# Second feed-forward layer of a four-layer model: first halves in four PSUM banks, second halves first, both products ahead of both clips

## What is computed

```python
def swiglu(x):
    g, l = jnp.minimum(x[..., ::2], 7.0), jnp.clip(x[..., 1::2], -7.0, 7.0)
    return g * jax.nn.sigmoid(1.702 * g) * (l + 1.0)
def body(acc, p):
    ew1, eb1, ew3, eb3, ew2, eb2, ce = p
    h = swiglu((xt @ ew1 + eb1) * (xt @ ew3 + eb3))
    return (acc + ce[:, None] * (h @ ew2 + eb2), None)
```

## Time and profile before

| | |
|---|---|
| median of the runs | 2266.28 us |
| the profiled execution, its span | 2269.38 us, 2267.8 us |
| busy over the span: TensorE, VectorE, ScalarE, GpSimd | 79%, 74%, 47%, 37% |
| first pass of the shared expert, last addition of the stage | 955.6 us, 1284.7 us |
| VectorE busy in that stretch | 301.1 us |
| TensorE busy in it | 288.8 us |
| granted TensorE clock: span, routed experts | 0.89, 1.00 |

### The profile page before, as it was taken

How to read it: one execution, slowest core, us unless ns; L and a number is a source line. 1 busy time by engine, 2 the same in 40 slices (tenths; PEclk the granted TensorE clock), 3 DMA queues, 4 the chain that set the end, 5 groups by cost and what they waited for, 6 DMA issues and landing times. The chain is left out here.

```text
span 2267.8 us, 46290 instructions
## 1 busy us (share of the span) xinstructions
PE 1800.0 (79%) x16408; PEld 1306.8 (58%) x16408; DVE 1674.2 (74%) x3948; ACT 1071.9 (47%) x2023; POOL 838.7 (37%) x632
## 2 busy tenths in 40 slices
PE   6999965888888975499999567878887659997756
PEld 3777742555555643377777434555554448886544
DVE  5999996776666757789999846988999672224674
ACT  4888843455545422144444324555565323332532
POOL 3000017755555401134443343455444219911111
PEclk8999987999999997699999867988898769998877
DMA  3111102000000000100000174444444250000000
GB/s 117 54 53 45 59 14 77 18 18 18 18 18 17 18 1 5 25 12 13 24 23 12 20 240 130 145 150 145 156 150 142 65 213 20 19 0 7 1 1 21
DMA packets 130613, 129.41 MB, mean 57 GB/s; under 512 B 76565, under 2 KB 107131, under 8 KB 129682
## 3 DMA queue, kind: packets, MB, share of 16 engines
q1 hardware_dynamic: 129522, 126.78, 18.8%
q10 hardware_dynamic: 928, 0.47, 0.1%
HBM read 78.59 MB, written 40.81 MB: 53 GB/s over the span
## 5 line engine op out<-in xcount | busy, mean ns | idle before, releaser
L2825 ACT ACTIVATE l2a_pr<-l2a_ps_s,l2a_nm 128x512 f32<-128x512 f32 x256 | 174.1, 686 | 140.9 <-DVE l2a_nm L2748 138.3
L529 ACT ACTIVATE l0a_pr<-l0a_sm,l0a_nm 128x512 f32<-128x512 f32 x256 | 185.0, 723 | 47.7 <-DVE l0a_nm L398 46.4
L398 DVE CUSTOM_DVE_ANT_0 l0a_sm<-l0a_ps_s,l0a_tb 128x512 f32<-128x512 f32 x256 | 174.9, 684 | 25.1 <-PE l0a_ps_s L613 18.5
L1703 POOL TENSOR_TENSOR l1f_h<-l1f_lm,l1f_sg 128x512 f32<-128x512 f32 x72 | 92.5, 1284 | 184.8 <-DVE l1f_lm L1767 184.8
L2748 DVE TENSOR_REDUCE l2a_nm<-l2a_ps_s 128x2 f32<-128x1024 f32 x128 | 156.7, 1224 | 4.4
L2755 DVE STREAM_TRANSPOSE l2a_tt<-l2a_pr 128x1024 f32<-128x1024 f32 x128 | 158.0, 1234 | 0.9 <-ACT l2a_pr L2825 0.8
L621 PE MATMUL l0a_ps_p<-top_c_ident,l0a_pr 128*128 128x128 f32 x1024 | 155.7, 274 | 0.0
L621 PEld LDWEIGHTS l0a_ps_p<-top_c_ident,l0a_pr 128*128 128x128 f32 x1024 | 129.0, 141 | 22.0 <-issue 0.9
L1829 ACT ACTIVATE l1f_csb<-l1f_ps_c,l1f_b3e 128x512 f32<-128x512 f32 x128 | 88.1, 689 | 107.5 <-PE l1f_ps_c L1615 107.3
L2082 ACT ACTIVATE l2f_h<-l2f_ps_h 128x512 f32<-128x512 f32 x128 | 76.5, 599 | 131.6 <-PE l2f_ps_h L1615 125.4
L2049 DVE SCALAR_TENSOR_TENSOR l2f_acc<-l2f_ps_y,l2f_comb,l2f_acc 128x128 f32<-128x128 f32 x112 | 31.5, 345 | 134.6 <-PE l2f_ps_y L2123 134.6
(11 more groups left out here) (535 smaller groups left out, 5098.8 us busy)
## 6 DMA issues: line engine op xcount, KB each, us to landing
l_qband<-l2a_staged SPq DMA_DIRECT2D x16, 768.0 KB, 16.2
l2a_qb<-l_qband SPq DMA_DIRECT2D x16, 768.0 KB
l2a_sb<-l_pband SPq DMA_DIRECT2D x32, 384.0 KB
l0a_tb<-l_bias SPq DMA_DIRECT2D x16, 448.0 KB
l2a_ks<-l_k SPq DMA_DIRECT2D x16, 384.0 KB
l_pband<-l2a_pr SPq DMA_DIRECT2D x32, 192.0 KB, 8.1
l_pband<-l2a_pr SPq DMA_DIRECT2D x32, 144.0 KB, 2.4
l2f_upw<-in_L_ffn_up_weights SPq DMA_DIRECT2D x9, 512.0 KB, 11.2
```

Source lines behind the costliest of these rows:

```text
L398: v.tensor_tensor_reduce(sm[j % 4][:, :], ps_s[j % 2][:, :], tb[slot][:, off:off + N][:, ::-1], -1.0, 3e38, ALU.add, ALU.min, nm[:, j % 4: ...
L529: a.activation(pr[j % 4][:, :], sm[j % 4][:, :], ACT.Exp, bias=nm[:, j % 4:j % 4 + 1], scale=-1.0).then_inc(m["p_ready"], 1)
L2825: a.activation(pr[slot][:, 2 * (g % 2) + u, :], ps_s[g % 2][:, u, :], ACT.Exp, bias=nm[:, g % 2, u:u + 1], accum_out=rs[:, n % 2, 2 * (g % ...
```

## The change

TensorE makes `c` first, then `a`; each has its own semaphore. `ps_a` gets four banks (one for each quarter), `ps_c` keeps two, `csb` gets four tiles. The two banks come from `ps_t` and `ps_g`, which now lie in the banks of `ps_y`. `c` of quarter m waits for the bias copy of quarter m - 2, `a` for the product of quarter m - 4. VectorE makes the products of both quarters of a half, then both clips, then the combine. ScalarE copies one half ahead: half 1 of batch b, sigmoid of half 0, half 0 of batch b + 1, sigmoid of half 1. Its loop runs over experts 1 to 6 now (three rounds), and 0, 7 and 8 are written out.

```diff
-        csb = [s.sb(f"csb{i}", [P, N]) for i in range(2)]
+        csb = [s.sb(f"csb{i}", [P, N]) for i in range(4)]
...
-        ps_a = [s.ps(f"ps_a{i}", [P, N]) for i in range(2)]
+        ps_a = [s.ps(f"ps_a{i}", [P, N]) for i in range(4)]
...
-        ps_y = [s.ps(f"ps_y{i}", [P, NT, D]) for i in range(2)]
-        ps_t = s.ps("ps_t", [P, N])
-        ps_g = s.ps("ps_g", [P, T, 32])
+        bank_y = [s.ps(f"ps_y{i}", [P, N]) for i in range(2)]
+        ps_y = [bank[:, :].rearrange("p (t d) -> p t d", d=D) for bank in bank_y]
+        ps_g, ps_t = bank_y[0][:, :].rearrange("p (t e) -> p t e", t=T), bank_y[1][:, :]
...
                 def gate(e, b):
...
+                    for k in range(2):
+                        for u in range(2):
+                            q = 2 * k + u
+                            v.wait_ge(csb_ready, n * 4 + q + 1)
+                            v.wait_ge(a_ready, n * 4 + q + 1)
...
+                            v.scalar_tensor_tensor(out=(lm if u else gm)[:, k, :], in0=ps_a[q][:, :],
+                                                   scalar=b1[:, e, k, u:u + 1], in1=csb[q][:, :],
+                                                   op0=ALU.add, op1=ALU.mult).then_inc(prod_done, 1)
+                        v.wait_ge(prod_done, n * 4 + 2 * k + 1)
+                        v.tensor_scalar(gm[:, k, :], gm[:, k, :], GLU_LIMIT, None, ALU.min).then_inc(gm_ready, 1)
+                        v.wait_ge(prod_done, n * 4 + 2 * k + 2)
+                        v.tensor_scalar(lm[:, k, :], lm[:, k, :], GLU_LIMIT, -GLU_LIMIT, ALU.min, ALU.max).then_inc(gl, 1)
...
+                def biased(e, b, k, bias):
+                    for u in range(2):
+                        q = 2 * k + u
+                        m = (e * B + b) * 4 + q
+                        a.wait_ge(c_ready, m + 1)
+                        if not (isinstance(m, int) and m < 4):
+                            a.wait_ge(prod_done, m - 3)
+                        a.activation(csb[q][:, :], ps_c[u][:, :], ACT.Identity, bias=bias[:, k, u:u + 1]).then_inc(csb_ready, 1)
...
+                def expert(e, bias, after, final=False):
+                    if not final:
+                        a.copy(after[:, :, :], b3[:, e + 1, :, :]).then_inc(b3e_ready, 1)
+                    for b in range(B):
+                        biased(e, b, 1, bias)
+                        sigmoid(e, b, 0)
+                        if b < B - 1:
+                            biased(e, b + 1, 0, bias)
+                        elif not final:
+                            a.wait_ge(b3e_ready, e + 1)
+                            biased(e + 1, 0, 0, after)
+                        sigmoid(e, b, 1)
...
                     for q, (k, u) in enumerate(halves):
                         m = n * 4 + q
...
                         if not (isinstance(m, int) and m < 2):
-                            pe.wait_ge(prod_done, m - 1)
...
+                            pe.wait_ge(csb_ready, m - 1)
+                        passes(1, ps_c[u]).then_inc(c_ready, 1)
+                        if not (isinstance(m, int) and m < 4):
+                            pe.wait_ge(prod_done, m - 3)
+                        passes(0, ps_a[q]).then_inc(a_ready, 1)
```

More of the change, by code:

```diff
@@ L1654, in l1_ffn @@
         b2_zero, b2_loaded = s.sem("b2_zero"), s.sem("b2_loaded")
-        ac_ready, csb_ready, prod_done, gm_ready, sg_ready = s.sem("ac_ready"), s.sem("csb_ready"), s.sem("prod_done"), s.sem("gm_ready"), s.sem("sg_ready")
+        a_ready, c_ready, csb_ready, prod_done, gm_ready, sg_ready = s.sem("a_ready"), s.sem("c_ready"), s.sem("csb_ready"), s.sem("prod_done"), s.sem("gm_ready"), s.sem("sg_ready")
         h_ready, y_ready, acc_done, dve, gl = s.sem("h_ready"), s.sem("y_ready"), s.sem("acc_done"), s.sem("dve"), s.sem("gl_done")
@@ L1749, in gate @@
                     n = e * B + b
[L1750 to L1768, removed]
@@ new lines, in gate @@
+                    for k in range(2):
[3 more added lines that the diff above has]
+                            v.wait_ge(a_ready, n * 4 + q + 1)
+                            if not (isinstance(n, int) and n == 0):
+                                if u:
+                                    v.wait_ge(h_ready, n * 2 + k - 1)
+                                else:
+                                    v.wait_ge(sg_ready, n * 2 + k - 1)
+                            v.scalar_tensor_tensor(out=(lm if u else gm)[:, k, :], in0=ps_a[q][:, :],
[5 more added lines that the diff above has]
+                        v.tensor_scalar(lm[:, k, :], lm[:, k, :], GLU_LIMIT, -GLU_LIMIT, ALU.min, ALU.max).then_inc(gl, 1)
+                        v.wait_ge(gl, n * 2 + k + 1)
+                        v.wait_ge(gm_ready, n * 2 + k + 1)
+                        v.scalar_tensor_tensor(out=lm[:, k, :], in0=lm[:, k, :], scalar=1.0, in1=gm[:, k, :],
+                                               op0=ALU.add, op1=ALU.mult).then_inc(hp, 1)
@@ L1820, in _ @@
                 a.wait_ge(biases, 16 * 2 * (E + 1))
-                def step(e, b, bias):
-                    n = e * B + b
[L1824 to L1846, removed]
+                def biased(e, b, k, bias):
[6 more added lines that the diff above has]
+                        a.activation(csb[q][:, :], ps_c[u][:, :], ACT.Identity, bias=bias[:, k, u:u + 1]).then_inc(csb_ready, 1)
@@ new lines, in sigmoid @@
+                def sigmoid(e, b, k):
+                    n = e * B + b
+                    a.wait_ge(gm_ready, n * 2 + k + 1)
+                    if not (isinstance(n, int) and n == 0):
+                        a.wait_ge(h_ready, n * 2 + k - 1)
+                    a.activation(sg[:, k, :], gm[:, k, :], ACT.Sigmoid, scale=GLU_ALPHA).then_inc(sg_ready, 1)
+                def expert(e, bias, after, final=False):
[10 more added lines that the diff above has]
+                        sigmoid(e, b, 1)
+                        if b == 0 and isinstance(e, int) and e == 0:
+                            a.wait_ge(ct_ready, 1)
+                            a.copy(combT[:, :], ps_t[0:R, :]).then_inc(combT_ready, 1)
@@ L1848, in _ @@
+                biased(0, 0, 0, b3[:, 0, :, :])
+                expert(0, b3[:, 0, :, :], b3e[0])
+                with a.Fori(0, E // 2 - 1) as i:
+                    expert(i * 2 + 1, b3e[0], b3e[1])
+                    expert(i * 2 + 2, b3e[1], b3e[0])
+                expert(E - 1, b3e[0], b3e[1])
+                expert(E, b3e[1], None, True)
             @block.tensor
@@ L1860, in up, with passes @@
                         m = n * 4 + q
+                        cols, rows = slice(k * H + u, (k + 1) * H, 2), slice(b * N, (b + 1) * N)
+                        def passes(i, bank):
+                            return three_passes(pe, bank[:, :], w13_high[slot][:, i, cols], w13_low[slot][:, i, cols],
+                                                r.zT_high[:, rows], r.zT_low[:, rows])
                         if not (isinstance(m, int) and m < 2):
-                            pe.wait_ge(prod_done, m - 1)
[L1863 to L1867, removed]
+                            pe.wait_ge(csb_ready, m - 1)
[3 more added lines that the diff above has]
+                        passes(0, ps_a[q]).then_inc(a_ready, 1)
                 def down(e, b, slot):
```

## The result

The changed kernel takes 2228.6 us, median of four runs (2223.95 to 2231.06); the kernel before 2266.57 (four runs, 2262.83 to 2269.59). The ratio is 0.983, with a 95% interval of 0.981 to 0.985: 38 us less, where 34 were forecast. The profiled execution took 2231.06 us, its span is 2229.3 (2267.8 before).

What follows compares the result with a forecast made beforehand. TensorE and VectorE, both almost full, were held in a product-passes-copy loop with TensorE one pair ahead at most. Start 8.0, experts 23.0 and tail 3.0 sum to 34.0 us saved, giving 2232 us; range 2223 to 2254.

Steps and rivals of the forecast that it cites:

- Floors: Least time per expert in the middle: TensorE 29.5 us, VectorE 29.5 us with the new order, 2.76 us per VectorE half.
- Seven experts: Middle of the stage: each routed expert falls from 33.69 to 30.4 us, together 23.0 us saved.
- The blocks: VectorE instructions in batch 2 stretched by GpSimd's weight split: three clips and the combine, up to 2.3 us an expert.
- The schedule of batch 2: Timeline of the batch with mask and weight split: clips held behind three splits, last multiply S + 13.9, TensorE losing 0.9 us.
- The recovery: After batch 2, VectorE, 3 us late, wins back 0.8 us a batch and is level by the next batch 2.
- Start: Stage's beginning: TensorE's 3.87 us stand shrinks to about 0.3, first down-projection 6.5 us earlier, shared batches 1.5; together 8.0 us.
- Tail: After expert 7, where VectorE sets the time: three faster gates and fewer waits for ScalarE, 3.0 us saved.
- Hidden at nothing: Shared banks for gating and transposes, weight loads and the next expert's bias copy were claimed to cost no time.
- Rival 1: VectorE stays the bound through port collisions or no overlap: expert 31.3 to 33.4 us, time 2240 to 2258, chance 0.26.
- Rival 2: GpSimd starved behind the late sigmoid, down-projection 1.2 us late in every batch: 5 us slower, 2271, chance 0.07.
- Rival 3: Another engine's order, ScalarE's, gives back what the banks give, start included: 2264 to 2269 us, chance 0.05.
- Rival 4: No stall in batch 2, all experts at 29.5 us: 2225 us, chance 0.04 for this and beyond.

## Why the prediction was right, and where not

The forecast was 2232 us; 2228.6 were measured, inside its range. By its steps:

- **Floors.** TensorE's 29.5 us an expert was exact: 29.51 and 29.52 in the two kernels in which nothing holds it up. A half on VectorE is 2.71 us against 2.76.
- **Seven experts**: 7 x (33.69 - 30.02) = 25.7 us, forecast 23.0. This term was mis-sized. The forecast let TensorE lose 0.9 us in batch 2; it loses about 0.5 (30.02 - 29.52). Its working was off in ways that partly cancel, so part of the closeness is luck. The blocks were taken at up to 2.3 us and are 3.07. But the mask costs 0.67 instead of 0.96: in the earlier trace rows it took 1.04 because it met GpSimd's multiply (1116.70 to 1118.00 in that trace), and it takes 0.75 now that the multiply comes later. The schedule of batch 2 went wrong at one seam:

```profile
1124.76 0.48 PE L1613 MATMUL l1f_ps_c<-l1f_zT_low,l1f_w_high 128*128 128x512 f32 x1
...
1138.18 2.05 PE L1902 MATMUL l1f_ps_y<-l1f_w,l1f_h 128*128 128x128 f32 x16 [0.21 <-POOL l1f_h L1703]
```

  With S = 1124.76 the products of half 0 end at S + 4.8 (forecast 5.3) and batch 1's multiply at S + 5.1 (5.25). So the first clip is already waiting when the multiply ends, goes ahead of the split and ends at S + 5.4, where the forecast had it behind the split's first part, at 6.8. The combine ends at S + 8.5 (9.65), the last multiply at S + 13.4 (13.9), and the down-projection starts right behind it; TensorE's batch is 7.86 us instead of 7.38. The recovery was foreseen about right: VectorE's gates start 5.6, 4.2 and 3.35 us behind TensorE's passes in the three batches after batch 2, and 3.3 is where they were before it.
- **Start**: 33.7 us are gained by the last addition of expert 7, 33.7 - 25.7 = 8.0 of them outside the seven periods. 0.8 of that lies before the stage's first pass and is no work of the change, so the start gains 7.2 where 8.0 were forecast. The first down-projection comes 14.7 us behind the first pass (21.5 before, 15.0 forecast). The 3.87 us stall of TensorE is gone, and with it the fall of the granted clock. In the trace before, the clock had risen to 1.00 by 960 to 962; TensorE then made no matmul from 962 to 964, and from 964 to 967 it was granted 0.50, the 1.2 GHz level. Now it works through and the clock stays at 1.00, the 2.4 GHz level (columns as in the earlier trace rows; the first line is the kernel before):

```profile
964.00:967.00 3.00, 2.95 (x7) 2.38 (x8) 2.21 (x4) 0.63 (x1) 0.62 (x1) 0.50 0.00 0
```
```profile
962.00:964.00 2.00, 1.89 (x11) 1.49 (x11) 1.75 (x5) 1.50 (x2) 0.00 (x0) 1.00 0.00 0
964.00:966.00 2.00, 2.00 (x10) 1.59 (x9) 1.97 (x5) 1.78 (x3) 0.68 (x1) 1.00 0.00 0
```

- **Tail**: 36.4 - 33.7 = 2.7 us, forecast 3.0. The waits of the earlier trace rows for bias copies do not appear any more.
- **Hidden at nothing**: shared banks, weight loads, the satisfied waits. No wait of VectorE or TensorE for any of them appears, and a product starts 0.66 us behind the one before it although it passes two semaphores, so the 0.2 us kept for satisfied waits were not needed. The two further copies were not priced apart; they are worth 1.0 us.
- So 25.7 + 2.7 + 7.2 = 35.6 in the stage. The 2.9 us by which the rest of the program was shorter in this pair of profiles are no effect that the runs could show; they lie within the scatter.

**The mechanism was incomplete.** The forecast said that the banks free TensorE from its pair-by-pair loop in every batch. The runs show a division of labour that it did not have: with second halves first, two banks already give ordinary batches at 7.4 to 7.6 us; the four banks serve batch 2 almost alone, as run-ahead across it; and they do so only if VectorE, by its new order, is faster than TensorE between slow batches. Per expert, from 33.69: second halves first -1.1, product order alone -0.6, second halves with banks and copies still -1.1 in all, second halves with the order and two banks still -1.1, everything -3.7. The four banks and the product order are each worth nothing without the other and 2.6 us with it, given second halves first. Four banks with first halves first were not run, so what the order of the halves is worth within the whole change is not shown.

**The rivals.** Rival 1 (VectorE stays the bound) gave an expert of 31.3 to 33.4; it fell, but one of its two signs, "VectorE busy over 97%", was there all the same: 98.5% in the middle. It was a bad sign to name, since VectorE's floor and blocked time fill the period in every variant. Its other sign decided: the mean first clip from 1136.67 to 1156.45, outside batch 2, is 0.48 us (six of them), far from 0.7. Rival 2 (GpSimd starved) fell: the down-projection waits once in four batches, 0.3 us at most on TensorE. Rival 3 (nothing moves) fell with the ratio of 0.983: the start and every expert are shorter. Rival 4 (no stall in batch 2, 29.5) is what the cast on ScalarE gives inside the stage, though not in the time.

## What to carry over

In this kernel, buffers that let the producer run ahead across a periodic slow iteration paid only when the consumer was faster than the producer in the iterations between. Find the slow one first, and check that surplus before adding banks. Parts of such a change tested one by one can each come out as nothing. Where two engines share a port, busy time doesn't say who bounds the loop: read the producer's gaps, and look for instructions that end a fixed time behind the other engine's.

## What the runs showed of the hardware that was not expected

- The stretch goes both ways. Between back-to-back GpSimd instructions of the split VectorE gets one clip or combine in, and GpSimd's next is then longer: L1707 takes 1.46 us instead of 1.28, L1709 1.50 instead of 1.25. That fits the lock on the shared ports which the Trainium skill describes ("SBUF — State Buffer", Who interferes with whom).
- VectorE's mask of two 128x512 pieces was stretched from 0.75 to 1.04 us as well, by a multiply that ended 0.43 us after it began: its row before the change had such a collision in it, unnoticed.
- The same code outside the stage took 1930 to 1939 us, while the stage repeats within 0.1.
